# Middle layers of a four-part transformer: probabilities divided on GpSimd before they are turned, and new work orders

## The reference

```python
h = shift_token(x); qkv = h @ wqkv                   # 8 heads of 64
q = l2norm(q) * qs; k = l2norm(k) * ksc              # then rotary_xpos
sim = einsum('bhwid,bhwjd->bhwij', bq * 8.0, bk)     # 128 queries, 256 keys: window before and own
attn = softmax(where(mask, -max, sim), axis=-1)
out = einsum('bhwij,bhwjd->bhwid', attn, bv)
x = x + out @ wo
h = layernorm(shift_token(x)) @ w1 + b1              # a, g = halves
x = x + (a * gelu(g)) @ w2 + b2
```

## Time and profile before

| | before |
|---|---|
| median of 3 runs (lowest to highest) | 2621.67 us (2618.68 to 2624.2) |
| time of the profiled execution | 2619.7 us |
| its span, first to last instruction | 2617.9 us |
| mean granted TensorE clock | 0.969 |
| busy: PE, DVE, ACT, POOL | 2478.5, 1992.0, 1616.4, 1111.2 us |

### The profile page before, as it was taken

How to read it: one execution, slowest core, us unless ns; L and a number is a source line. 1 busy time by engine, 2 the same in 40 slices (tenths; PEclk the granted TensorE clock), 3 DMA queues, 4 the chain that set the end, 5 groups by cost and what they waited for, 6 DMA issues and landing times. The chain is left out here.

```text
span 2617.9 us, 57926 instructions
## 1 busy us (share of the span) xinstructions
PE 2478.5 (95%) x20386; PEld 2245.2 (86%) x20386; DVE 1992.0 (76%) x5970; ACT 1616.4 (62%) x3738; POOL 1111.2 (42%) x969
## 2 busy tenths in 40 slices
PE   7999999978999999999999999999669999899997
PEld 6999999977899999988889999999658887788886
DVE  6899999857888888888888888887366556755554
ACT  4788888836877877877878778778245113431111
POOL 3232333225455455455454554453145334533332
PEclk7999999989999999999999999999789999999999
DMA  2011221122222222233322222222332012221111
GB/s 79 24 36 36 93 68 50 33 77 73 85 87 80 89 87 82 88 99 100 108 84 90 86 82 88 87 80 90 102 111 84 34 33 85 89 73 33 33 33 41
DMA packets 223622, 190.39 MB, mean 73 GB/s; under 512 B 22373, under 2 KB 205801, under 8 KB 222313
## 3 DMA queue, kind: packets, MB, share of 16 engines
q1 hardware_dynamic: 204616, 177.04, 21.3%
q10 hardware_dynamic: 18720, 9.64, 1.3%
HBM read 91.13 MB, written 44.04 MB: 52 GB/s over the span
## 5 line engine op out<-in xcount | busy, mean ns | idle before, releaser
L2153 ACT ACTIVATE c_kern_hi<-c_kern 128x512 fp32r<-128x512 f32 x128 | 81.1, 634 | 365.4 <-DVE c_kern L2275 365.4
L1372 ACT ACTIVATE b_sb_probs<-b_sb_probs,b_sb_neg_top,b_sb_r_norm 128x256 f32<-128x256 f32 x512 | 301.7, 595 | 3.1 <-DVE b_sb_neg_top L1510 2.3
L2056 POOL TENSOR_TENSOR c_kern_lo<-c_kern,c_kern_hi 128x512 fp32r<-128x512 f32 x128 | 171.9, 1344 | 292.0 <-ACT c_kern_hi L2153 292.0
L1277 POOL TENSOR_TENSOR b_sb_r_norm<-b_sb_squares,b_sb_power 128x8 f32<-128x8 f32 x64 | 105.1, 1642 | 353.8 <-DVE b_sb_squares L1460 353.8
L39 PE MATMUL psum<-b_sb_fT_lo,b_sb_w_hi 128*128 128x256 f32 x768 | 224.4, 292 | 13.2 <-DVE b_sb_mid L1572 6.5
L41 PE MATMUL psum<-b_sb_fT_hi,b_sb_w_hi 128*128 128x256 f32 x768 | 217.1, 283 | 0.0
L40 PE MATMUL psum<-b_sb_fT_hi,b_sb_w_lo 128*128 128x256 f32 x768 | 216.9, 282 | 0.0
L1503 DVE CUSTOM_DVE_ANT_0 b_sb_probs<-psum,b_sb_mask 128x256 f32<-128x256 f32 x512 | 195.3, 419 | 11.9 <-DVE b_sb_mid L1572 10.6
L39 PE MATMUL psum<-c_kern_lo,c_v_hi 128*128 128x512 f32 x512 | 204.3, 399 | 0.0
L41 PE MATMUL psum<-c_kern_hi,c_v_hi 128*128 128x512 f32 x512 | 200.5, 392 | 0.0
L40 PE MATMUL psum<-c_kern_hi,c_v_lo 128*128 128x512 f32 x512 | 200.4, 392 | 0.0
(11 more groups left out here) (311 smaller groups left out, 8928.4 us busy)
## 6 DMA issues: line engine op xcount, KB each, us to landing
b_sb_kT_hi<-b_sb_kT_hi SPq DMA_DIRECT2D x64, 256.0 KB, 2.8
b_sb_kT_lo<-b_sb_kT_lo SPq DMA_DIRECT2D x64, 256.0 KB, 3.0
b_sb_v_prev<-b_sb_v_now SPq DMA_DIRECT2D x64, 256.0 KB, 2.4
Y<-b_sb_y SPq DMA_DIRECT2D x128, 128.0 KB, 2.1
b_sb_res<-Y SPq DMA_DIRECT2D x64, 128.0 KB, 2.1
b_sb_x_f<-Y SPq DMA_DIRECT2D x128, 64.0 KB, 1.9
b_sb_res_f<-Y SPq DMA_DIRECT2D x64, 128.0 KB, 2.3
U<-c_u_out SPq DMA_DIRECT2D x16, 512.0 KB, 4.0
```

The source lines that it names most:

```text
L1277: pool.tensor_tensor(r, s, p, ALU.pow).then_inc(r_ready[1][b], 1)
L1372: ins = act.activation(probs[b][:, n, :], probs[b][:, n, :], ACT.Exp, bias=neg_top[b][:, n:n + 1], scale=r_norm[b][:, h:h + 1], accum_out= ...
L2056: pool.tensor_tensor(kern_lo[i % RING][:], kern[i % RING][:], kern_hi[i % RING][:].bitcast(F32), ALU.subtract)\
```

## The change

For the division by the row sums, the probabilities themselves are multiplied by the reciprocals on GpSimd, in place, after the exponentials and before the turning: two instructions of 128x512 for each half of the heads and each batch. The reciprocals are taken in halves (`invert`, `invert2`). With that `turn_r`, `spread_r` and the product in `values` go. The high part of the output is copied from PSUM directly, and VectorE takes the low part from PSUM, where GpSimd took it from SBUF. All five orders are new: below stand TensorE's and VectorE's whole, of the others what has to do with this.

```diff
-        "pe": [("up", 2, -4), ("turn_p", 1, -2), ("project_q", 0, -1), ("up", 3, -4), ("project_k", 1, -1),
-               ("turn_p2", 1, -2), ("bias", 0, -1), ("values", 0, -2), ("values", 1, -2), ("turn_r", 1, -2),
-               ("turn_r", 0, -2), ("up", 4, -4), ("project_q", 1, -1), ("project_v", 1, -1), ("project_v", 0, -1),
-               ("turn_qk", 0, -1), ("turn_h", 0, 0), ("up", 5, -4), ("turn_h", 1, 0), ("turn_f", 0, -3), ("out", 1, -2),
-               ("scores", 0, -1), ("scores2", 0, -1), ("turn_qk", 1, -1), ("down", 0, -4), ("up", 0, -3), ("up", 1, -3),
-               ("out", 0, -2), ("scores", 1, -1), ("scores2", 1, -1), ("turn_p", 0, -1), ("project_k", 0, 0),
-               ("down", 1, -4), ("turn_p2", 0, -1)],
+        "pe": [("project_q", 0, -1), ("up", 3, -4), ("turn_p", 1, -2), ("project_k", 1, -1), ("turn_p2", 1, -2),
+               ("values", 0, -2), ("values", 1, -2), ("project_q", 1, -1), ("project_v", 1, -1), ("turn_qk", 0, -1),
+               ("up", 4, -4), ("turn_h", 0, 0), ("project_v", 0, -1), ("up", 5, -4), ("turn_f", 0, -3), ("turn_h", 1, 0),
+               ("out", 1, -2), ("scores", 0, -1), ("scores2", 0, -1), ("turn_qk", 1, -1), ("out", 0, -2), ("up", 0, -3),
+               ("bias", 0, -1), ("up", 1, -3), ("down", 0, -4), ("scores", 1, -1), ("scores2", 1, -1), ("down", 1, -4),
+               ("project_k", 0, 0), ("turn_p", 0, -1), ("up", 2, -3), ("turn_p2", 0, -1)],
+        "dve": [("turn_p", 0, -1), ("up", 2, -3), ("sums_q", 0, 0), ("turn_p", 1, -1), ("spin_q", 0, 0),
+                ("moments", 0, -2), ("mid", 1, -3), ("up", 3, -3), ("sums_k", 1, 0), ("turn_o", 0, -1), ("spin_k", 1, 0),
+                ("norm", 0, -2), ("swap_f", 5, -3), ("turn_o", 1, -1), ("mid", 2, -3), ("sums_q", 1, 0), ("spin_q", 1, 0),
+                ("swap_f", 1, -2), ("swap_f", 2, -2), ("turn_qk", 0, 0), ("up", 4, -3), ("mid", 3, -3), ("turn_h", 0, 1),
+                ("turn_f", 0, -2), ("out", 1, -1), ("up", 5, -3), ("turn_h", 1, 1), ("mid", 4, -3), ("scores", 0, 0),
+                ("turn_qk", 1, 0), ("mid", 5, -3), ("scores2", 0, 0), ("up", 0, -2), ("invert", 0, 0), ("out", 0, -1),
+                ("down", 0, -3), ("swap_f", 0, -1), ("scores", 1, 0), ("up", 1, -2), ("invert2", 0, 0), ("scores2", 1, 0),
+                ("invert", 1, 0), ("swap_f", 3, -2), ("down", 1, -3), ("bias", 0, 0), ("sums_k", 0, 1), ("swap_f", 4, -2),
+                ("mid", 0, -2), ("spin_k", 0, 1), ("invert2", 1, 0)],
...
+        "sp": [("values", 0, 3), ("swap", 0, 5), ("swap", 4, 1), ("swap_f", 3, 2), ("scores2", 0, 3), ("scores2", 1, 3),
+               ("values", 1, 3), ("swap_f", 0, 3), ("swap_f", 4, 2), ("swap_f", 1, 3), ("swap", 1, 5), ("down", 1, 0),
...
+        "pool": [("scale", 1, 3), ("scale2", 1, 3), ("swap", 2, 4), ("project_k", 0, 4), ("moments", 0, 2),
+                 ("project_q", 0, 4), ("project_k", 1, 4), ("swap", 3, 3), ("project_q", 1, 4), ("swap", 0, 5),
+                 ("load_r", 0, 1), ("swap", 4, 1), ("swap", 1, 5), ("rope", 0, 5), ("scale", 0, 4), ("scale2", 0, 4)],
...
-            def turn_o(t, b):
-                pool.wait_ge(o_hi_ready[b], t + 1)
-                pool.tensor_tensor(oT_lo[b][:], oT[b][:], oT_hi[b][:].bitcast(F32), ALU.subtract).then_inc(o_lo_ready[b], 1)
+            def scaled(t, b, half):
+                pool.wait_ge(r_sum_ready[b], 2 * t + half + 1)
+                for m in (2 * half, 2 * half + 1):
+                    p = probs[b][:, 2 * m:2 * m + 2, :]
+                    pool.tensor_tensor(p, p, r_sum[b][:, 2 * m:2 * m + 2, None].broadcast_to([P, 2, 2 * P]), ALU.mult)\
+                        .then_inc(p_scaled[b], 1)
...
-            def spread_r(t, b):
...
-            def turn_r(t, b):
...
             def turn_o(t, b):
-                act.wait_ge(o_ready[b], t + 1)
+                ring.wait_full(act, t, ("o", b))
                 ring.wait_last_full(act, t, ("wo", b))
-                act.activation(oT_hi[b][:], oT[b][:], ACT.Copy).then_inc(o_hi_ready[b], 1)
+                act.activation(oT_hi[b][:], ring.out(t, ("o", b), 512).rearrange("p (c q) -> p c q", c=pairs), ACT.Copy)\
+                   .then_inc(o_hi_ready[b], 1)
...
+            def inverted(t, b, half):
+                part = slice(4 * half, 4 * half + 4)
+                dve.wait_ge(p_ready[b], 4 * t + 2 * half + 2)
+                dve.wait_ge(p_scaled[b], 4 * t)
+                dve.reciprocal(r_sum[b][:, part], row_sum[b][:, part]).then_inc(r_sum_ready[b], 1)
...
+            def turn_o(t, b):
+                dve.wait_ge(o_hi_ready[b], t + 1)
+                ring.read(t, dve.tensor_tensor(oT_lo[b][:], ring.out(t, ("o", b), 512).rearrange("p (c q) -> p c q", c=pairs),
+                                               oT_hi[b][:].bitcast(F32), ALU.subtract), ("o", b))
...
             def turned_p(t, b, ms):
                 for m in ms:
-                    pe.wait_ge(p_ready[b], t * 4 + m + 1)
+                    pe.wait_ge(p_scaled[b], t * 4 + m + 1)
```

More of the change, by code:

```diff
@@ L933, in layer_b @@
     order = {
[L934 to L942, removed]
@@ L950, in layer_b @@
[L950 to L958, removed]
@@ L959, in layer_b @@
[L959 to L963, removed]
@@ L964, in layer_b @@
-        "pool": [("project_q", 0, 3), ("swap", 2, 3), ("moments", 0, 1), ("swap", 4, 0), ("turn_o", 1, 2),
-                 ("project_k", 1, 3), ("load_r", 0, 0), ("project_q", 1, 3), ("turn_o", 0, 2), ("rope", 0, 4),
-                 ("swap", 0, 4), ("swap", 3, 3), ("swap", 1, 4), ("project_k", 0, 4)],
+        "act": [("scores", 0, 0), ("up", 0, -2), ("up", 1, -2), ("swap_f", 0, -1), ("scores2", 0, 0), ("scores", 1, 0),
+                ("project_k", 0, 1), ("mid", 0, -2), ("scores2", 1, 0), ("swap", 2, 1), ("up", 2, -2), ("project_q", 0, 1),
+                ("swap_f", 1, -1), ("turn_p2", 0, 0), ("swap", 3, 0), ("turn_p2", 1, 0), ("mid", 1, -2),
+                ("project_k", 1, 1), ("up", 3, -2), ("turn_o", 0, 0), ("turn_o", 1, 0), ("swap", 0, 2),
+                ("project_q", 1, 1), ("swap_f", 5, -2), ("mid", 2, -2), ("swap_f", 2, -1), ("load", 1, 2),
+                ("project_v", 1, 1), ("up", 4, -2), ("swap", 1, 2), ("mid", 3, -2), ("swap_f", 3, -1), ("turn_qk", 0, 1),
+                ("up", 5, -2), ("project_v", 0, 1), ("turn_h", 0, 2), ("turn_f", 0, -1), ("turn_h", 1, 2), ("load", 0, 3),
+                ("swap_f", 4, -1), ("swap", 4, -2), ("mid", 4, -2), ("mid", 5, -2), ("turn_qk", 1, 1)],
@@ L1035, in layer_b @@
         r_sum = [sb(f"r_sum{b}", [P, B_HEADS]) for b in both]
-        oT = [sb(f"oT{b}", [P, pairs, P]) for b in both]
         oT_hi = [sb(f"oT_hi{b}", [P, pairs, P], F32R) for b in both]
@@ L1060, in layer_b @@
                 "scores": ["s0", "s1"], "scores2": ["s2", "s3"], "turn_p": ["p0", "p1"], "turn_p2": ["p2", "p3"],
-                "turn_r": ["r"], "values": ["o"], "out": ["wo"]}
+                "values": ["o"], "out": ["wo"]}
         jobs.update(turn_f=["f"], up=["w"], down=["y"], bias=["bias"])
@@ L1442, in _ @@
                                        "project_v": project_v, "turn_qk": turn_qk, "scores": scores, "scores2": scores2,
-                                       "turn_p2": turn_p2, "spread_r": spread_r, "turn_r": turn_r, "turn_o": turn_o, "turn_f": turn_f, "up": up, "mid": mid_})
+                                       "turn_p2": turn_p2, "turn_o": turn_o, "turn_f": turn_f, "up": up, "mid": mid_})
         @block.vector
@@ L1607, in _ @@
                                        "turn_qk": turn_qk, "scores": scores, "scores2": scores2, "turn_p": turn_p,
-                                       "turn_r": turn_r, "values": values, "out": out,
+                                       "invert": invert, "invert2": invert2, "turn_o": turn_o, "out": out,
                                        "moments": moments, "norm": norm, "turn_f": turn_f, "up": up, "mid": mid_,
@@ L1700, in turn_p2 @@
                 turned_p(t, b, (2, 3))
-            def turn_r(t, b):
-                pe.wait_ge(r_wide_ready[b], t + 1)
-                ring.wait_bank(pe, t, ("r", b))
-                for c in range(pairs):
-                    ins = pe.transpose(ring.out(t, ("r", b), 512)[:, c * P:(c + 1) * P],
-                                       oT[b][:, c, :], ident[:])
-                ring.written(t, ins, ("r", b))
             def values(t, b):
@@ L1770, in _ @@
                                       "project_v": project_v, "turn_qk": turn_qk, "scores": scores, "scores2": scores2,
-                                      "turn_p": turn_p, "turn_p2": turn_p2, "turn_r": turn_r, "values": values, "out": out,
+                                      "turn_p": turn_p, "turn_p2": turn_p2, "values": values, "out": out,
                                       "turn_f": turn_f, "up": up, "down": down})
```

39 lines of the change are left out of this document (15 added, 24 removed).

## The result

| | before | after |
|---|---|---|
| median (lowest to highest), 4 runs each | 2620.66 us (2618.68 to 2624.2) | 2595.53 us (2594.59 to 2599.31) |
| ratio, 95% interval | | 0.9905 (0.9888 to 0.9923) |
| span of the profiled execution | 2617.9 us | 2594.4 us |

What follows compares the result with a forecast made beforehand. It took TensorE to bound the kernel before, and a VectorE-ScalarE loop of 38.5 us (35.7, locks 2.6, waits 0.2) the changed one: 2619.7 - 28 x 0.45 (12.6) + 2 = 2609 us, range 2585 to 2640.

Steps and rivals of the forecast that it cites:

- TensorE's own order is the bound: Middle layers of the kernel before: TensorE, busy 38.74 of a 38.95 us step, was said to bound it, by little.
- if TensorE is at 99% again, my loop is wrong: Sign to check afterwards: TensorE's busy time was expected 0.5 us or more under the step's length.
- 2.5 us are all the room it has: VectorE in the kernel before: of 5.6 us idle a step, only waits for gate (1.4) and outputs (0.9 + 0.2) counted.
- worth nothing by itself: ScalarE losing the turned factors' two instructions for both batches, some 2.5 us a step; claimed gain nothing, since nobody waited.
- TensorE alone 37.75: TensorE's own step length after the change: 38.95 less 1.30 for eight transposes, plus 0.10 for regrouping, 37.75 us.
- Locks 2.6 us: VectorE standing under GpSimd's two-operand instructions in the changed kernel: 2.6 us a step, or 3.4 to 3.6, for 2.2 before.
- the second rival: GpSimd's sum beats VectorE at mid 2, 1.25 us lock, loop 39.3, 2631 us; 0.30 together with longer multiplications.
- Loop without locks 35.7: New loop from VectorE's up 0 through scores 0 and ScalarE to next up 0: 30.0 plus 5.74 us.
- level, within 0.2 us: VectorE's work: subtraction for product, four reciprocals for two (0.2 us each more), against two gaps gone; no net change.
- The first rival: TensorE stays the bound at 37.75 us a step, locks under 2.0 us; 33.6 us less, 2588 us; chance 0.18.
- SyncE's queue at nothing, up to 0.5 us: Key copies issued between the value copies ScalarE's project_v waits for; priced nothing, up to 0.5 us a step if later.
- Weight steps within 5 us, ends + 2: Steps where weights change: 5 us either way; first and last step about 1 us longer each, 2 together.

Runs made afterwards that it cites:

- e1: Changed kernel with one extra VectorE operation (about 0.33 us a step) in the second half of batch 1's scores: 2600.92 us, 0.9940 of the kernel before.
- e3: Changed kernel without the output projection's products with the low half of the weights (0.94 us less TensorE a step): 2590.25 us, 0.9903 of the kernel before.
- e11: Changed kernel, SyncE's key copies ahead of the value copies, low-half output weight products left out (TensorE - 0.94 us): 2578.89 us, 0.9853 of the kernel before.
- e13: Kernel before, without the output projection's products with the low half of the weights (0.94 us less TensorE a step): 2620.20 us, ratio 1.0001.
- e17: Kernel before, ScalarE's two copies of batch 0's turned probabilities moved behind the gelu of up 2: 2614.11 us, ratio 0.9977, step 38.64 us.
- e7: Changed kernel, VectorE's middle tile 2 low half ahead of batch 1's low outputs, SyncE's key copies ahead of value copies: 2575.45 us, 0.9825 of the kernel before.
- e10: Changed kernel, SyncE's key copies ahead of the value copies, eight transposes a step done twice: 2596.08 us, 0.9921 of the kernel before.
- e18: Kernel before, turned-probability copies behind the gelu of up 2, low-half output weight products left out (TensorE - 0.94 us): 2606.90 us, ratio 0.9951, step 38.64 us.
- e9: Changed kernel with only SyncE's four key copies put ahead of the two value copies: 2580.71 us, 0.9863 of the kernel before, all steps 37.78 us.

## Why the prediction was wrong, by its steps

Two steps failed. In the sum it is the length of the new loop: 38.5 us were forecast, 37.78 measured. That VectorE and ScalarE bound the changed kernel was right (e1, e3, e11); the size was not. And for the kernel before, TensorE was not the bound (e13), so that the prediction could not say where the gain comes from.

- *"TensorE's own order is the bound"*: this step failed, and with it the use of the number 37.75. It rested on 38.74 busy us of 38.95. e13 took 0.94 us off TensorE and the step moved by 0.02, with its busy time still at 38.35, 0.39 less. Busy 99% was not slack zero. For the same reason the sign "if TensorE is at 99% again, my loop is wrong" misled: it was at 99.9%, and the loop was the bound.
- *"2.5 us are all the room it has"*: 1.4 us of these were the waits for the gate, which I took for room of VectorE. 1.03 of them was the loop's own path through ScalarE. The chain had to be followed past the end of the earlier trace rows, to up 2, not up 0.
- *ScalarE "worth nothing by itself"*: two copies moved behind up 2 are worth up to 0.98 us a step by the traces, most of the gain, and 0.31 by the run that moved them alone (e17). The prediction looked at the four table loads only.
- *TensorE alone 37.75*: 37.56 (e7). Eight transposes more cost 0.87 (e10); that they stand in a group there and not by themselves makes this no exact measure of the forecast 1.2. But the kernel before with its transposes ran at 38.64 us without TensorE as its bound (e17, e18), so TensorE's own length there is 38.64 at most, and the saving 1.08 at most. They were not what bounded the kernel before, but the whole gain could not have been had with them: with the key copies first e10's step is 38.43 us, 0.52 under the one before.
- *The multiplications*, 1.03 us, 25 us of GpSimd a step, hardly a wait for them: right.
- *Locks 2.6 us*: 2.45, by two errors that cancel. Mid 0 did not stand (0.41 at 1571.34; the forecast was 0.95 more), VectorE got in between the two multiplications. At mid 2 GpSimd came first, as in the second rival, for 1.04 instead of 0.25. That the sum was near is luck.
- *Loop without locks 35.7*: the term that was mis-sized. From up 0 at 1563.16 to the end of the next step's first L1505, 1595.19, are 32.03 us, less 2.45 of locks, so 29.6 for the forecast 30.0; ScalarE's part 5.74 as forecast; the waits for turned halves 0 for 0.2. VectorE's own work is thus 29.6 + 4.2 = 33.8 us a step, where 34.2 were carried over from the kernel before: its part was not "level, within 0.2 us" but 0.4 us shorter. Together with the locks the loop was 0.7 us too long, 16 us over 22 steps. The first rival's time, 2588, came near for another reason than its own.
- *28 full steps*: 22. By itself that would have made the forecast 2612, 3 us further off.
- *SyncE's queue at nothing, up to 0.5 us*: not nothing, but inside its bound. The late copy made two steps 1.95 us longer, some 5 us over the 22 full steps; e9 is faster by 15 us, the rest of which is not shown to be the copy's.
- *Weight steps within 5 us, ends + 2*: the weight steps, - 1.6, were right. The ends came to + 0.4, near by luck: 4.8 lost ahead of the first step, 4.8 gained in the last three, 0.5 lost in the tail.
